# Attention row maxima: a custom VectorE operation with an added mask in place of mask products on TensorE

## The reference, cut to what matters

```python
scores = jnp.einsum('bqhd,bkhd->bhqk', qq, kk) * scale      # 16 heads, 16 numbers each
causal = jnp.tril(jnp.ones((S, S), dtype=bool))             # S = 512
scores = jnp.where(causal[None, None], scores, jnp.finfo(scores.dtype).min)
probs = jax.nn.softmax(scores, axis=-1)
y = jnp.einsum('bhqk,bkhd->bqhd', probs, v).reshape(B, S, H)
```

## Time and profile before

| | |
|---|---|
| median of the runs | 4385.75 us (3 runs, 4384.99 to 4388.7) |
| profiled execution, span | 4383.6 us, 2.2 us below the median of the runs |
| attention, slices 1 to 16 of 40 | about 0 to 1760 us |
| routed experts | about 1760 to 2100 us |
| Mamba branch | about 2100 to 4380 us |
| busy over the span | PE 86%, DVE 67%, ACT 57%, POOL 50% |
| TensorE's mean granted clock | 0.934 of full speed |

### The profile page before, as it was taken

One profiled execution on the slowest core, in us unless ns is written; L12 is line 12 of the kernel. 1 busy time (PEld: TensorE's weight loads), 2 busy tenths in 40 slices (PEclk: granted clock), 3 DMA queues, 4 the chain that ended last, 5 costly groups with the idle time before them and its releaser, 6 DMA issues.

```text
span 4383.6 us, 70750 instructions
## 1 busy us (share of the span) xinstructions
PE 3756.6 (86%) x22264; PEld 2785.4 (64%) x22264; DVE 2958.8 (67%) x5456; ACT 2514.4 (57%) x6505; POOL 2196.1 (50%) x1115
## 2 busy tenths in 40 slices
PE   5888888888888883999869888998999999989987
PEld 2344444444444442777758787887887887887876
DVE  3444454545444532222269999999999999999998
ACT  1433343434433441333368887887887887887874
POOL 3223333333333322000048877877778778778775
PEclk7889999999998996999989999999999999999998
DMA  3322222322232213666622222222222222222221
GB/s 99 91 76 84 80 84 87 94 80 79 93 97 81 88 41 99 201 210 209 198 88 76 97 84 76 93 88 76 93 88 76 93 88 76 93 86 78 93 78 42
DMA packets 286603, 419.96 MB, mean 96 GB/s; under 512 B 78262, under 2 KB 250679, under 8 KB 263673
## 3 DMA queue, kind: packets, MB, share of 16 engines
q1 hardware_dynamic: 273048, 381.12, 26.5%
q0 software_dynamic: 12288, 33.57, 2.2%
q10 hardware_dynamic: 864, 0.10, 0.0%
HBM read 330.63 MB, written 83.17 MB: 94 GB/s over the span
## 4 chain that ended last, share of the span: by engine, by line
DVE 33%; issue 11%; PE 2%; ACT 2%; DVEq 1%; POOL 1%; DMA 0%; SPq 0%; POOLq 0%; ACTq 0%
DVE m_S L1756 7%; DVE m_PR L1756 7%; DVE m_S L1748 7%; DVE m_PR L1748 7%; ACT m_dA L1645 1%; DVE m_ub L1733 1%; DVE m_yz L1767 1%; PE m_F L1866 1%; DVE m_x L1717 1%; DVE m_th_x L1725 1%; DVEq L1747 1%; PE m_Y L1904 1%; POOL m_ub L1536 0%; PE m_F L1864 0%; PE m_F L1840 0%
## 5 line engine op out<-in xcount | busy, mean ns | idle before, releaser
L1536 POOL TENSOR_TENSOR m_ub<-m_Bb,m_dtx 128x2048 f32<-128x2048 f32 x254 | 1156.3, 4564 | 321.4 <-PE m_Y L1904 219.6
L1645 ACT ACTIVATE m_dA<-m_dt,m_a_neg 128x128 f32<-128x128 f32 x4096 | 1211.1, 388 | 132.2 <-DVE m_S L1756 131.8
L1904 PE MATMUL m_Y<-m_ub,m_ident 128*128 128x128 f32 x8192 | 972.3, 281 | 90.6 <-DVE m_ub L1733 90.4
L1904 PEld LDWEIGHTS m_Y<-m_ub,m_ident 128*128 128x128 f32 x8192 | 955.5, 197 | 102.0 <-DVE m_ub L1733 102.0
L543 ACT ACTIVATE f_pt<-f_X 128x512 f32<-128x512 f32 (+1 forms) x704 | 371.3, 555 | 735.1 <-PE f_X L845 696.6
L618 DVE TENSOR_REDUCE f_nm<-f_Y 128x1 f32<-128x512 f32 (+3 forms) x896 | 434.4, 531 | 366.9 <-PE f_Y L845 342.6
L1748 DVE SCALAR_TENSOR_TENSOR m_PR<-m_dA,m_S 128x512 f32<-128x512 f32 x512 | 355.8, 695 | 54.4 <-issue 29.9
L1748 DVE SCALAR_TENSOR_TENSOR m_S<-m_dA,m_PR 128x512 f32<-128x512 f32 x512 | 354.8, 693 | 12.0
L1756 DVE CUSTOM_DVE_ANT_1 m_PR<-m_PR,m_ub 128x512 f32<-128x512 f32 x512 | 353.4, 690 | 9.9 <-issue 9.8
L1756 DVE CUSTOM_DVE_ANT_1 m_S<-m_S,m_ub 128x512 f32<-128x512 f32 x512 | 353.3, 690 | 0.0
L828 PE MATMUL f_Y<-f_kst,f_qst 96*128 96x512 bf16 (+3 forms) x1024 | 258.4, 333 | 109.2 <-DVE f_nm L618 90.9
(11 more groups left out here) (234 smaller groups left out, 6365.7 us busy)
## 6 DMA issues: line engine op xcount, KB each, us to landing
m_Bb<-m_bc_dram SPq DMA_DIRECT2D x64, 1024.0 KB, 4.5
m_Cb<-m_bc_dram SPq DMA_DIRECT2D x64, 1024.0 KB, 6.2
f_parts_dram<-f_parts SPq DMA_DIRECT2D x32, 768.0 KB, 4.0
f_kst<-f_parts_dram SPq DMA_DIRECT2D x192, 128.0 KB, 2.6
f_qst<-f_parts_dram SPq DMA_DIRECT2D x192, 128.0 KB, 2.6
e_rows<-sorted_rows SPq DMA_DIRECT2D x70, 256.0 KB, 2.7
e_wg<-Wg SPq DMA_DIRECT2D x70, 256.0 KB, 2.9
e_wu<-Wu SPq DMA_DIRECT2D x70, 256.0 KB, 3.9
```

The source lines that it names most:

```text
L1536: pool.tensor_tensor(ub[:, h, i, :, :], Bb[:, s, :, :], dtx[:, m, None, s * SN:(s + 1) * SN].to_broadcast([P, NST, SN]), ALU.mult).then_in ...
L1645: last = act.activation(dA[:, h, i, n, :], dtt[:, par, m, s * SN:(s + 1) * SN], ACT.Exp, scale=a_neg[:, m, n:n + 1])
L1904: last = pe.matmul(Y[:, i * SN:(i + 1) * SN], ident[:, :], ub[:, h, 1 + i, n, :], start=False, stop=(n == NST - 1), skip_group_check=True)
```

## The change

The mask products of the first pass go. The score products signal the full bank themselves. VectorE's row maximum becomes `tensor_tensor_reduce`: it reads the bank, adds a bf16 tile `f_causal` (zeros, with the triangle of -1e30 in its last 128 columns, so that the last `n` columns are the mask for a row of `n` scores), multiplies by -1, writes that back in place into the bank, and keeps the minimum, which an instruction of its own writes to `f_nm`. Every row maximum now has one row of scores, so the bank with two heads takes two of them: eight for a pair. The wait for the full bank is taken once per bank, with an increment of a semaphore that nobody waits for. The tile `f_th` goes, ScalarE's tanh writes into `f_sg` and VectorE combines in place; the wait for the previous reader of `f_sg` moves from VectorE to ScalarE.

```diff
--- before.py
+++ after.py
@@ -60,7 +60,7 @@
     rope = sb("f_rope", [P, 2, SEQ])
     ident = sb("f_ident", [P, P])
     identb = sb("f_identb", [P, P], bf16)
-    mask_q = sb("f_mask_q", [P, P], bf16)
+    causal = sb("f_causal", [P, SEQ], bf16)
     mask_k = sb("f_mask_k", [P, P], bf16)
     tri = sb("f_tri", [P, P], bf16)
     onesb = sb("f_onesb", [P, P], bf16)
@@ -120,8 +120,8 @@
     run_ = sb("f_run", [P, ER])
     info = sb("f_info", [P, TT, 2 * TOPK])
     info_i = info[:, :, :].bitcast(i32)
-    th = sb("f_th", [P, NS, SEQ])
     sg = sb("f_sg", [P, NS, SEQ])
+    th = sg
     hm = sg
     sums_dram = nc.dram_tensor("f_sums_dram", [PAIRS, HG, 2, SEQ], f32).ap()
     shares_dram = nc.dram_tensor("f_shares_dram", [PAIRS, HG, 2, SEQ], f32).ap()
@@ -438,8 +438,8 @@
             fixed(pool.memset(identb[:, :], 0.0))
             fixed(pool.affine_select(out=identb[:, :], in_=identb[:, :], compare_op=ALU.not_equal, fill=1.0,
                                      base=0, pattern=[[-1, P]], channel_multiplier=1))
-            fixed(pool.memset(mask_q[:, :], 0.0))
-            fixed(pool.affine_select(out=mask_q[:, :], in_=mask_q[:, :], compare_op=ALU.is_ge, fill=MASKED,
+            fixed(pool.memset(causal[:, :], 0.0))
+            fixed(pool.affine_select(out=causal[:, SEQ - P:SEQ], in_=causal[:, SEQ - P:SEQ], compare_op=ALU.is_ge, fill=MASKED,
                                      base=0, pattern=[[-1, P]], channel_multiplier=1))
             fixed(pool.memset(mask_k[:, :], 0.0))
             fixed(pool.affine_select(out=mask_k[:, :], in_=mask_k[:, :], compare_op=ALU.is_ge, fill=MASKED,
@@ -603,7 +603,7 @@
             if kind == "g":
                 act.wait_ge(*filled(("g", i), r))
                 if not isinstance(b, int) or b > 0:
-                    act.wait_ge(*used(("g", i), before_(r)))
+                    act.wait_ge(*filled(("d", 1), before_(r)))
                 act.activation(th[:, i, :], bank_of(("g", i), r)[:, :], ACT.Tanh, scale=0.5).then_inc(th_ready, 1)
         run(nc.scalar, do)
 
@@ -614,8 +614,13 @@
             return bank_of(k, r)
 
         def do(kind, i, j, b, r):
-            def row_max(k, out, cols, last=True):
-                ins = dve.tensor_reduce(out, cols(full(k, r)), AX.X, ALU.max, negate=True)
+            def row_max(k, out, c0, n, last=True):
+                if c0 == 0:
+                    dve.wait_ge(*filled(k, r))
+                    dve.sem_inc(taken)
+                cols = bank_of(k, r)[:, c0:c0 + n]
+                ins = dve.tensor_tensor_reduce(out=cols, in0=cols, in1=causal[:, SEQ - n:SEQ], scale=-1.0, scalar=-MASKED,
+                                               op0=ALU.add, op1=ALU.min, accum_out=out)
                 if last:
                     ins.then_inc(free_sem(k, r), 1)
             p = parity(kind, r)
@@ -648,12 +653,15 @@
                 h = 2 * i
                 if i == 0 and j == 0:
                     dve.wait_ge(nm_step, 5 * b)
+                if isinstance(b, int) and b == 0:
+                    dve.wait_ge(const_ready, N_CONST)
                 if j < 2:
-                    row_max(("s1", i, j, 0), nm[:, 3, h + j:h + j + 1], lambda bank: bank[:, :])
-                    row_max(("s1", i, j, 1), nm[:, 2, h + j:h + j + 1], lambda bank: bank[:, 0:384], last=False)
-                    row_max(("s1", i, j, 1), nm[:, 0, h + j:h + j + 1], lambda bank: bank[:, 384:512])
+                    row_max(("s1", i, j, 0), nm[:, 3, h + j:h + j + 1], 0, 512)
+                    row_max(("s1", i, j, 1), nm[:, 2, h + j:h + j + 1], 0, 384, last=False)
+                    row_max(("s1", i, j, 1), nm[:, 0, h + j:h + j + 1], 384, 128)
                 else:
-                    row_max(("s1", i, j, 0), nm[:, 1, h:h + 2], lambda bank: bank[:, :].rearrange("p (h n) -> p h n", h=2))
+                    row_max(("s1", i, j, 0), nm[:, 1, h:h + 1], 0, 256, last=False)
+                    row_max(("s1", i, j, 0), nm[:, 1, h + 1:h + 2], 256, 256)
             if kind == "mvx":
                 dve.wait_ge(sc_step, 10 * b + 8)
                 dve.wait_ge(xn_done, 2 * b)
@@ -742,9 +750,6 @@
                 dve.wait_ge(slot_step, SL * b + 4)
                 dve.tensor_copy(info_i[:, :, 0:TOPK].rearrange("p j k -> p k j"), oh[:, :, :, 0]).then_inc(slot_step, 1)
             if kind == "g":
-                if i == 0 and (not isinstance(b, int) or b > 0):
-                    dve.wait_ge(*filled(("d", 1), before_(r)))
-                    dve.sem_inc(taken)
                 bank = full(("g", i), r)
                 dve.wait_ge(th_ready, NS * b + i + 1)
                 dve.scalar_tensor_tensor(sg[:, i, :], th[:, i, :], 1.0, bank[:, :], ALU.add, ALU.mult).then_inc(free_sem(("g", i), r), 1)
@@ -825,8 +830,8 @@
         def scores(bank, c0, h, qb, p):
 
             n = P * (qb + 1)
-            pe.matmul(bank[:, c0:c0 + n], qst[p][0:KS, h, qb * P:(qb + 1) * P], kst[p][0:KS, h, 0:n],
-                      start=(c0 == 0), stop=False, skip_group_check=True)
+            return pe.matmul(bank[:, c0:c0 + n], qst[p][0:KS, h, qb * P:(qb + 1) * P], kst[p][0:KS, h, 0:n],
+                             start=(c0 == 0), stop=True, skip_group_check=True)
 
         def scores_t(bank, c0, h, kb, p):
 
@@ -868,17 +873,14 @@
                     pe.wait_ge(stacked[i // 4], 16 * NSTACK * (b + 1))
                 if j < 2:
                     bank = free(("s1", i, j, 0), r)
-                    scores(bank, 0, h + j, 3, p)
-                    full(("s1", i, j, 0), r, hide(bank, 384, P, 1, mask_q))
+                    full(("s1", i, j, 0), r, scores(bank, 0, h + j, 3, p))
                     bank = free(("s1", i, j, 1), r)
                     scores(bank, 0, h + j, 2, p)
-                    scores(bank, 384, h + j, 0, p)
-                    full(("s1", i, j, 1), r, hide(bank, 256, P, 2, mask_q))
+                    full(("s1", i, j, 1), r, scores(bank, 384, h + j, 0, p))
                 else:
                     bank = free(("s1", i, j, 0), r)
                     scores(bank, 0, h, 1, p)
-                    scores(bank, 256, h + 1, 1, p)
-                    full(("s1", i, j, 0), r, hide(bank, P, 2 * P, 2, mask_q))
+                    full(("s1", i, j, 0), r, scores(bank, 256, h + 1, 1, p))
             if kind == "nmt":
                 bank = free(("nmt",), r)
                 pe.wait_ge(nm_step, 5 * (b + 1))
```

## The result

The changed kernel takes 4391.94 us (median of 10 runs, 4383.23 to 4407.03), the kernel before, run beside it, 4380.9 us (median of 10, 4366.06 to 4388.7). The ratio is 1.003 with a 95% interval of 1.0016 to 1.0044: slower by 0.3%, which is 13 us by the ratio and 11 us by the two medians. The forecast was 13 us slower. The profile shows that this agreement is an accident of two large differences with opposite signs.

A forecast was written before the change was run, and what follows sets the result against it. Attention was taken as paced by TensorE's and VectorE's waits on two rings of two banks. VectorE adds 2.6 us a round, TensorE gives back 1.8: 13 us in 16 rounds on 4385.75, about 4398 us; range 4350 to 4442.

The forecast's parts named there:

- VectorE's part: Attention's row maxima: custom operations, splits and write-outs add 5.9 us a round, 2.6 of it on the path.
- The write-out: Instruction writing each row maximum's minimum out in the attention: 0.083 us each, 64 a round, 5.3 us a round.
- the custom operation itself costs the same: VectorE's row maximum in attention: 690 ns for 512 elements against the reduction's 684, no difference taken for PSUM.
- the split: Two-head bank in attention: two operations of 256 at 416 ns replace one of 512, adding 0.55 us a round.
- rival B: Attention: write-outs pass beside their operations and TensorE's saving arrives; 24 to 34 us faster, 4352 to 4362 us; chance 26%.
- set-off of the separate wait against the earlier signal: Attention's banks: signalled full 0.06 to 0.11 us earlier, the separate wait with increment costs about that; taken as cancelling.
- Rival A: Attention: each write-out waits for its operation and costs 0.164 us; 50 us slower, 4435 us; chance 20%.
- TensorE's part: Attention's first pass: removing the mask products saves 3.8 us a round, of which 1.8 reaches the end.
- at the stretch's granted clock of 0.92 I count 3.8 us a round: Attention: the removed masks' 3.5 us a round of TensorE time, converted at that clock; 61 us in 16 rounds.
- Rival C: Attention: missing products and longer waits lower TensorE's clock to 0.90; 32 us on top, 4430 us; chance 8%.
- Experts and Mamba should keep their 340 and 2280 us: Stages outside the attention: the change leaves the experts' 340 us and the Mamba branch's 2280 us as they were.
- what would show it: Profile tests for the attention: round of 100.5 to 102.5 us, TensorE busy about 110 us less in ten rounds.

The follow-up runs named there:

- dve_alone: The changed kernel with the first pass's mask products kept and 105 increments holding the Mamba loop's old place; 4405.26 us, ratio 1.0071 to the kernel before.
- wait_inc: The kernel before, reductions kept, with the change's separate wait and increment once per bank, Mamba loop's place kept; 4378.47 us, ratio 1.0019.
- before_more: The kernel before with 151 increments moving VectorE's Mamba loop, and useless products of the masks' shapes beside the masks; 4358.6 us, ratio 0.997.
- pe_alone: The kernel before without the first pass's mask products, queries scaled by 0.01, VectorE's reductions unchanged; 4427.2 us, ratio 1.0121.
- pe_front: The kernel before with useless identity products ahead of the scores in place of the first pass's masks, queries scaled by 0.01; 4372.15 us, ratio 1.0003.
- after_front: The changed kernel with useless products of the removed masks' shapes and 105 increments holding the Mamba loop's old place; 4401.99 us, ratio 1.0069 to the kernel before.
- after_pad: The changed kernel with 105 increments putting VectorE's Mamba loop back at its old place within a block; 4434.22 us, ratio 1.0131 to the kernel before.

## Why the prediction was right in total and wrong in its parts

**VectorE's part, direction right, terms wrong.** The forecast was 42 us: 5.9 us a round, of which 2.6 on the path. The long stretch holds 156 / 16 = 9.75 rounds, and VectorE is busy for 517.15 / 9.75 = 53.0 us in each, where it was 50.2: 2.9 us more, half of the 5.9. Two terms were off, in opposite directions. The write-out, with 5.3 us a round the largest, adds nothing between two operations: it passes beside the one that follows, and the next still starts 0.083 us before the end of the one ahead. The row that I took its price from holds small instructions that follow one another, and there each costs its 0.083 us. The other term is "the custom operation itself costs the same", which held for 512 elements alone. The groups of 384 and 128 take 591 and 332 ns where the reductions took 550 and 281; with the 700 against 684 that is 0.108 us a head, 1.7 us a round. Two groups of 256 take 451 ns each, not 416: with the overlap 2 x 0.368 us in place of 0.602, so the split costs 1.1 us a round and not 0.55. These two make 2.8 of the 2.9 us. So rival B's condition, a write-out that passes beside its operation, held, and the longer operations, which it didn't have, kept B from coming true.

On the path dve_alone shows 31 us, 1.9 us a round. My set-off of the separate wait against the earlier signal failed as well: in wait_inc the wait costs 0.5 us of these. For the remaining 1.4 us there is an estimate: a bank is released with the write-out, which ends 0.06 us behind its operation, and with 12.6 releases a round that is up to 0.8 us; the rest would be the longer operations. No run shows this division. Rival A, the write-out at its whole length between two operations, is excluded by the rows in order of time.

**TensorE's part, wrong in sign.** The forecast was 29 us back, from 1.8 us a round. The products' own time may well have been right: before_more pays 1.5 us a round for as many, though no run changes their number at a constant clock. But removing them costs 53 us alone, and about 27 us on top of VectorE's part (1.0131 against 1.0069 and 1.0071). The step that failed is "at the stretch's granted clock of 0.92 I count 3.8 us a round": it kept the clock constant under a change of what TensorE does. Rival C named the mechanism and had it at 8%, with a fall to 0.90. It fell to 0.87 and 0.85. By the same rule of conversion the fall from 0.92 to 0.86 in pe_alone costs up to 6 us of 101 a round, 97 us in 16 rounds; less the 29 us that I had counted as saved that is 68, and 53 were measured. The price, an upper bound, held; the size of the fall and its chance did not. The evidence was in the earlier trace rows and in my own text: a stretch at 0.92 spends 16% of its time at the lower of the two levels, so it sits on the slope, where work taken from TensorE can tip more of it down. That should have given C far more than 8%.

"TensorE: Matmul & The Clock Gate", part 1, in the Trainium skill says that the array's default is the throttled clock and that activity releases it. pe_front and after_front agree: products with no use bring the clock from 0.86 to 0.93 and from 0.85 to 0.92. That a kernel can gain by leaving them in, the runs show and I had not drawn from it.

**"Experts and Mamba should keep their 340 and 2280 us", wrong.** The Mamba branch lost 38 us. The step that is missing counts what the change does to the programs of the engines outside the changed code. 663 instructions more on VectorE moved a loop that nobody had edited. The row that would have warned stood at the head of the same view as the earlier trace rows:

```profile
L1748 DVE SCALAR_TENSOR_TENSOR m_PR<-m_dA,m_S 128x512 f32<-128x512 f32 x512 | 355.8, 695 | 54.4 <-issue 29.9 <-POOL m_ub L1536 6.3 <-ACT m_dA L1645 1.9
```

I looked there for the price of a custom operation and passed over 29.9 us of idle time that nothing in the profile explains, since the change was in the attention.

**The sum.** For the change with the loop's place held, the forecast was +13 us and after_pad shows about +57 (31 for VectorE, 27 for TensorE). The Mamba loop took back about 40. The forecast of 4398 us, the range and the "slower" came true with two wrong terms that cancel. Of the tests in "what would show it" two did speak at once: a round of 104.8 us is beyond the 103 at which I wanted the clock looked at, and TensorE's busy time didn't fall by 110 us in ten rounds but stayed, 85.9 us a round in place of 85.8.

**The alias**: nothing, as forecast.

## What to carry to other kernels

Before you take cheap products from TensorE, look at the granted clock of the stretch: where it lies between its two levels, each product also holds up the clock of all others, and taking products away can cost more than they took; try a useless product of the same shape to see which it is. Count the instructions that a change adds to each engine ahead of any later loop, and look for waits for issue behind that loop's branch: a shift of some hundred instructions moved an untouched stage by 1.7% of its time, and a few increments of an unused semaphore do the same on purpose. And when a total comes out as forecast, compare stage by stage before you believe the reasons.

## What the runs showed of the hardware

An accumulator's write-out on VectorE lasts 142 ns, starts together with the next operation, some 0.08 us before its own operation ends, and adds no time between two operations; behind the last of a row it ends 0.06 us after its operation. The custom operation that adds a bf16 tile, writes back into PSUM and keeps a minimum takes 700, 591, 451 and 332 ns for 512, 384, 256 and 128 elements; the reductions take 684, 550 and 281 ns for 512, 384 and 128. VectorE stands for about 2.8 us behind the branch of its Mamba loop of 367 instructions when the loop starts at 190 within a block of 256, and for 0.2 to 0.3 us when it starts at 84 or 85. ScalarE's Mamba loop, of the same length, goes from 0.2 to about 2.5 us when 60 instructions are put ahead of it. In the attention three engines stand for some 4 to 7 us each behind their branches at the same time; freeing one of them gained nothing.
